# One 512-column matmul for w2's rounded part and its remainder, in a mixture-of-experts kernel

## What is computed

```python
logits = x2d @ wg                     # 2048 tokens, 8 experts
gates = softmax(logits); idx = argmax(logits)
# each expert takes the first C = 256 tokens that chose it
h  = relu(einsum('ecm,emh->ech', di, w1))     # w1: 8 x 256 x 1024
eo = einsum('ech,ehm->ecm', h, w2)            # w2: 8 x 1024 x 256
out = t + combine(gates, eo)
```

## Time and profile before

| | us |
|---|---|
| median of 3 runs | 190.01 (190.01 to 190.08) |
| the profiled execution | 189.76 |
| its span | 187.9 |

### The profile page before, as it was taken

How to read it: one execution, slowest core, us unless ns; L and a number is a source line. 1 busy time by engine, 2 the same in 40 slices (tenths; PEclk the granted TensorE clock), 3 DMA queues, 4 the chain that set the end, 5 groups by cost and what they waited for, 6 DMA issues and landing times.

```text
span 187.9 us, 3937 instructions
## 1 busy us (share of the span) xinstructions
PE 175.9 (94%) x1370; PEld 168.8 (90%) x1370; DVE 147.6 (79%) x400; ACT 112.8 (60%) x273; POOL 119.6 (64%) x159
## 2 busy tenths in 40 slices
PE   7899999799999999989899899999999999999980
PEld 7788898699899999769899899999999999999970
DVE  1397979998987978755867889999699996997820
ACT  0647966578679488523659795791875926845000
POOL 4226778278877967828349688748468494369562
PEclk9999999999999999999999999999999999999996
DMA  5896997611312124769299629139184193601010
GB/s 169 244 368 226 301 258 205 234 61 58 112 36 85 58 86 124 244 179 304 53 330 356 236 79 390 36 127 345 62 284 162 63 348 145 205 22 45 5 68 30
DMA packets 23862, 31.67 MB, mean 169 GB/s; under 512 B 2729, under 2 KB 20650, under 8 KB 23841
## 3 DMA queue, kind: packets, MB, share of 16 engines
q1 hardware_dynamic: 20032, 26.01, 42.5%
q0 software_dynamic: 1616, 4.24, 6.4%
q10 hardware_dynamic: 2192, 1.16, 2.1%
HBM read 23.02 MB, written 8.55 MB: 168 GB/s over the span
## 4 chain that ended last, share of the span: by engine, by line
PE 65%; DVE 12%; DMA 10%; issue 5%; ACT 4%; SPq 2%; POOLq 1%; POOL 0%; DVEq 0%
PE banks_v L603 8%; PE banks_v L604 7%; PE banks_v L610 7%; DMA w_in_sb<-in_L_ffn_w 6%; PE banks_o L675 4%; PE bank_q L610 3%; PE bank_pT L610 3%; PE bank_pT L603 3%; PE bank_pT L604 3%; PE bank_s L610 3%; PE bank_s L603 3%; PE bank_s L604 3%; PE bank_q L603 3%; PE bank_q L604 3%; DMA slots<-row,slot 2%
## 5 line engine op out<-in xcount | busy, mean ns | idle before, releaser
L950 ACT ACTIVATE w_high<-w_in_sb 128x1024 fp32r<-128x1024 f32 x22 | 22.9, 1057 | 4.2 <-DMA w_in_sb<-in_L_ffn_w 4.0
L560 POOL DMA_INDIRECT out<-y,goal x16 | 16.7, 1041 | 11.6 <-issue 5.8
L483 POOL DMA_INDIRECT slots<-row,slot x14 | 14.3, 1023 | 14.7 <-DVE slot L1233 8.8
L542 POOL TENSOR_TENSOR w_low<-vx,w_high 128x1024 fp32r<-128x1024 f32 x8 | 20.1, 2532 | 5.2 <-ACT w_high L950 5.2
L542 POOL TENSOR_TENSOR w_low<-w_in_sb,w_high 128x1024 fp32r<-128x1024 f32 x7 | 16.7, 2409 | 9.7 <-ACT w_high L950 9.6
L1322 DVE TENSOR_TENSOR w_low<-w_in_sb,w_high 128x1024 fp32r<-128x1024 f32 x12 | 15.8, 1317 | 5.1 <-ACT w_high L950 4.7
L603 PE MATMUL banks_v<-w_high,h_high 128*128 128x256 f32 x64 | 16.3, 291 | 0.5 <-issue 0.5
L675 PE MATMUL banks_o<-vx,pT 128*128 128x266 f32 x64 | 16.4, 397 | 0.3 <-issue 0.3
L1048 ACT ACTIVATE h_high<-bank_xT 128x512 fp32r<-128x512 f32 x8 | 4.8, 594 | 18.6 <-PE bank_xT L610 18.6
L604 PE MATMUL banks_v<-w_high,h_low 128*128 128x256 f32 x64 | 15.8, 283 | 0.0
L603 PE MATMUL bank_pT<-w_high,h_high 128*128 128x256 f32 x56 | 14.0, 287 | 0.0
(11 more groups left out here) (239 smaller groups left out, 658.1 us busy)
## 6 DMA issues: line engine op xcount, KB each, us to landing
w_in_sb<-in_L_ffn_w SPq DMA_DIRECT2D x12, 1024.0 KB, 6.6
vx<-in_L_ffn_w SPq DMA_DIRECT2D x4, 1024.0 KB
sl<-slots SPq DMA_DIRECT2D x9, 266.0 KB, 4.2
slots<-empty SPq DMA_DIRECT2D x8, 266.0 KB, 4.1
sl<-in_x SPq DMA_DIRECT2D x8, 256.0 KB, 8.9
out<-row SPq DMA_DIRECT2D x7, 256.0 KB
table_in<-in_tables ACTq DMA_DIRECT2D x1, 292.0 KB, 8.3
w_in_sb<-in_L_conv_Wq ACTq DMA_DIRECT2D x1, 256.0 KB, 4.0
```

What stands on the lines that cost most here:

```text
L483: nc.gpsimd.indirect_dma_start(slot_rows, bass.IndirectOffsetOnAxis(ap=slot_of(i)[:, t:t + 1].bitcast(u32), axis=0), row_of(i)[:, t, :], N ...
L542: step = nc.gpsimd.tensor_tensor(w2_low[e % 2][:, half, :], w2_raw[e % 2][:, half, :], w2_high[e % 2][:, half, :].bitcast(f32), ALU.subtract)
L560: nc.gpsimd.indirect_dma_start(out_rows, bass.IndirectOffsetOnAxis(ap=goal[j][:, c:c + 1].bitcast(u32), axis=0), y[j][:, c, :], None, boun ...
L950: nc.scalar.activation(high[e % 2][:, half, :], raw[:, half, :], ACT.Copy).then_inc(ready, 1)
```

## The change

- w2's high and low parts lie in one buffer, row block by row block side by side (`w2_parts`), so that 512 neighbouring columns hold both.
- `expert_out` no longer uses `three_passes`. For each of the eight blocks it issues one matmul of 512 columns with the high part of h (it gives high x high in the left half of a bank and high x low in the right half), and one of 256 columns with the low part of h into the left half. In the last block the order of the two is turned round. Each tile of 128 tokens has a bank of its own, and the same two banks serve every expert, so the output of e waits for the eviction of e - 1 (`y_ready`).
- The eviction of experts 0 to 6 becomes four operations: for each tile y = right half x gate + own row, then a wait for both, then for each tile y = left half x gate + y.
- The last expert keeps the three passes, in `last_expert_out`; the bank of its second tile is another one.
- `gather_T(1)` stands ahead of the sixth block of expert 0's second tile, and the waits for h's remainders in its first tile stand ahead of the pair of blocks that uses them.

```diff
@@ -195,7 +195,9 @@
         xs = [sb(f"xs{j}", [P, 2, D]) for j in range(2)]
         xg_high, xg_low = ([sb(f"xg_{n}{j}", [P, DC, CAP], f32r) for j in range(2)] for n in ("high", "low"))
         w1_high, w1_low = ([sb(f"w1_{n}{j}", [P, DC, F], f32r) for j in range(2)] for n in ("high", "low"))
-        w2_high, w2_low = ([sb(f"w2_{n}{j}", [P, FC, D], f32r) for j in range(2)] for n in ("high", "low"))
+        w2_parts = [sb(f"w2_parts{j}", [P, FC, 2, D], f32r) for j in range(2)]
+        w2_high, w2_low = ([w[:, :, part, :] for w in w2_parts] for part in range(2))
+        w2_both = [w[:, :, :, :].rearrange("p c a d -> p c (a d)") for w in w2_parts]
         h_high, h_low = ([sb(f"h_{n}{j}", [P, FC, CAP], f32r) for j in range(2)] for n in ("high", "low"))
         y = [sb(f"y{j}", [P, 2, D]) for j in range(2)]
         goal = [sb(f"goal{j}", [P, 2], i32) for j in range(2)]
@@ -226,10 +228,10 @@
         ps_wo_wgc = ps_o[:, 0, 0:DC * EXTRA].rearrange("p (a b) -> p a b", a=DC)
 
         ps_h = [ps_xT, ps_q, ps_s, halves(ps_v[:, 0, :])]
-        ps_y = [halves(ps_v[:, 1, :]), ps_pT]
+        ps_y = [ps_v[:, 1, :], bank_pT[:, :]]
         ps_gT = [halves(ps_o[:, j, :]) for j in range(2)]
 
-        ps_y_last = [ps_gT[0][:, 0, :], ps_y[1][:, 1, :]]
+        ps_y_last = [ps_gT[j][:, 0, :] for j in range(2)]
 
         const_in, eye_in, weights_in, wv_in, small_in, wg_in, token_in = (sem(n) for n in (
             "const_in", "eye_in", "weights_in", "wv_in", "small_in", "wg_in", "token_in"))
@@ -843,21 +845,37 @@
 
             def expert_out(e):
 
-                j, last = e % 2, e == E - 1
+                j = e % 2
                 pe.wait_ge(w2_split, e + 1)
                 if e == 0:
                     pe.wait_ge(first_w2_low, 1)
                 else:
                     pe.wait_ge(h_split, (FC // 2) * (e + 1))
+                    pe.wait_ge(y_ready[1 - j], (e - 1) // 2 + 1)
                 for t in range(2):
                     own = slice(t * P, (t + 1) * P)
-                    step = three_passes(ps_y_last[t] if last else ps_y[j][:, t, :],
-                                        [(h_high[j][:, f, own], h_low[j][:, f, own]) for f in range(FC)],
-                                        [(w2_high[j][:, f, :], w2_low[j][:, f, :]) for f in range(FC)],
-                                        before_last=(lambda: gather_T(1)) if e == 0 and t == 1 else None,
-                                        before_pair=(lambda q: pe.wait_ge(h_split, q + 1)) if e == t == 0 else None)
-                    if last or t == 1:
-                        step.then_inc(y_made, 1)
+                    for f in range(FC):
+                        if e == 0 and t == 0 and f % 2 == 0:
+                            pe.wait_ge(h_split, f // 2 + 1)
+                        if e == 0 and t == 1 and f == FC - 3:
+                            gather_T(1)
+                        high, low, both = h_high[j][:, f, own], h_low[j][:, f, own], w2_both[j][:, f, :]
+                        if f < FC - 1:
+                            nc.tensor.matmul(ps_y[t], high, both, start=f == 0, stop=False)
+                        nc.tensor.matmul(ps_y[t][:, 0:D], low, w2_high[j][:, f, :], start=False, stop=False)
+                        if f == FC - 1:
+                            nc.tensor.matmul(ps_y[t], high, both, start=False, stop=True).then_inc(y_made, 1)
+
+            def last_expert_out():
+
+                e = E - 1
+                j = e % 2
+                pe.wait_ge(w2_split, e + 1)
+                pe.wait_ge(h_split, (FC // 2) * (e + 1))
+                for t in range(2):
+                    own = slice(t * P, (t + 1) * P)
+                    three_passes(ps_y_last[t], [(h_high[j][:, f, own], h_low[j][:, f, own]) for f in range(FC)],
+                                 [(w2_high[j][:, f, :], w2_low[j][:, f, :]) for f in range(FC)]).then_inc(y_made, 1)
 
             hidden(0)
             expert_out(0)
@@ -867,8 +885,7 @@
                 if e + 2 < E:
                     gather_T(e + 2)
                 expert_out(e)
-            pe.wait_ge(y_ready[1], E // 2 - 1)
-            expert_out(E - 1)
+            last_expert_out()
 
 
         @block.scalar
@@ -1337,14 +1354,24 @@
                 gate.done(nc.vector.tensor_tensor(gate_g[:, tiles(e)], ginv[:, tiles(e)], rstd_g[:, tiles(e)], ALU.mult))
                 dve.wait_ge(y_free, e + 1)
                 nc.vector.tensor_copy(goal[j][:, :], sl[:, tiles(e), COL_TOK]).then_inc(goal_ready, 1)
+                if last:
+                    for t in range(2):
+                        dve.wait_ge(y_made, 2 * e + t + 1)
+                        r = 2 * e + t
+                        nc.vector.scalar_tensor_tensor(y[j][:, t, :], ps_y_last[t], gate_g[:, r:r + 1], sl[:, r, 0:D],
+                                                       ALU.mult, ALU.add).then_inc(y_ready[j], 1)
+                    return
                 for t in range(2):
-                    if last or t == 0:
-                        dve.wait_ge(y_made, e + 1 + t)
+                    dve.wait_ge(y_made, 2 * e + t + 1)
                     r = 2 * e + t
-                    step = nc.vector.scalar_tensor_tensor(y[j][:, t, :], ps_y_last[t] if last else ps_y[j][:, t, :], gate_g[:, r:r + 1],
-                                                          sl[:, r, 0:D], ALU.mult, ALU.add)
-                    if last or t == 1:
-                        step.then_inc(y_ready[j], 1)
+                    gate.mark(nc.vector.scalar_tensor_tensor(y[j][:, t, :], ps_y[t][:, D:2 * D], gate_g[:, r:r + 1], sl[:, r, 0:D],
+                                                             ALU.mult, ALU.add))
+                gate.done()
+                for t in range(2):
+                    r = 2 * e + t
+                    step = nc.vector.scalar_tensor_tensor(y[j][:, t, :], ps_y[t][:, 0:D], gate_g[:, r:r + 1], y[j][:, t, :],
+                                                          ALU.mult, ALU.add)
+                step.then_inc(y_ready[j], 1)
 
             first_w2_piece(2)
 
```

## The result

The changed kernel takes 194.1 us (median) where the kernel before took 190.05: the ratio is 1.020, interval 1.015 to 1.025. A second set of runs gave 1.019 (1.011 to 1.027). The median is of four executions, of which one, 196.25 us, ran in a slower state and is left out of the ratio. The profiled execution takes 192.78 us with a span of 191.0, so 3.1 more than the 187.9 of before. It is slower, as forecast; by the ratio the loss is 3.8 us (0.020 x 190.05), where the forecast's sum was 2.6.

A forecast was written before the change was run, and what follows sets the result against it. A ring through DVE, SP, ACT and POOL, slower than PE, was taken as the bound: +0.2 and +2.7 at POOL's last subtraction, +2.6 at PE's start, 192.6 us; 191.5 to 193.7 at 70 in 100, wider range 190.6 to 194.4.

The forecast's parts named there:

- the ring: Loop through DVE's odd evictions, SP's loads, ACT's rounding and POOL's subtraction; a lap took 24.53 and 24.68 us, PE needs 23.90.
- five steps: DVE evicts; POOL's subtraction sets that start; SP's loads wait for the scatter; ACT waits for w1, rounds; POOL subtracts again.
- The eviction: On DVE, experts 0 to 6: two more operations and a wait, 1.76 us instead of 0.86, +0.90 an expert.
- Each odd eviction adds its whole 0.90: Evictions of experts 1, 3 and 5, no slack in the ring: +2.70 us at POOL's last subtraction.
- The start of the ring: First two experts, up to the ring's first step: +0.2 us taken, between ends of -0.6 and +0.9.
- The sum at POOL: End of POOL's last subtraction, for w2 of expert 7: 176.17 + 0.2 + 2.7 = 179.07.
- The wide matmul: PE's expert outputs: 512 columns take 0.2267 us, 0.347 with a narrow one; an expert saves 0.21 us.
- PE waits for POOL at expert 7: Before expert 7's output PE arrives at about 176.8, waits 2.3 us and starts at 179.1 instead of 176.54, +2.6.
- The wait for the banks: PE before expert e's output, for e - 1's eviction: fits for experts 1 to 5, about 0.6 us short for 6.
- PE's wait for the x remainder: At 105.64, behind expert 0's longer eviction on DVE: PE waits until about 106.1, +0.45 us.
- The clock: Rival: PE's idle gap before expert 7 lowers the clock, up to 5.1 us more, 193.7 to 197.7; 10 in 100.
- The even evictions cost nothing: Evictions of even experts stand outside the ring, so their longer time adds nothing at POOL's last subtraction.

The follow-up runs named there:

- second profile: The changed kernel run again without an edit and traced: 194.05 us median, ratio 1.019 (1.011 to 1.027); the profiled execution has a span of 193.0.

## Why the prediction was right, and where not

*The time: inside the range, above the sum.* The median of 194.1 lies between 190.6 and 194.4, but 1.5 above the 192.6 and outside the narrower 191.5 to 193.7. What the profiles show above the sum is the fall of the clock and, in the second, late landings in the ring; both are below. How the executions without a trace share in them is open. The 0.4 us that I gave as what a measurement can tell was too fine: 21 executions of the kernel before lie between 188.81 and 191.65.

*What bounds the kernel: right.* The ring was found in the rows of before, with its five steps. Cutting it at one place returned the kernel to 189.24, and adding only the second pair to the kernel before gave 192.87.

*The eviction: right.* 1.76 was forecast, 1.77 measured.

*Each odd eviction adds its whole 0.90: too much in this execution.* The laps grew by 0.54 and 0.67. Up to the scatter the 0.90 is there: from the eviction's start to the first scatter it took 145.59 - 142.94 = 2.65 us, and 144.44 - 142.70 = 1.74 in the trace of before. But the second scatter ended 1.52 us ahead of SP's loads (148.11 to 149.63), while in the trace of before it was 1.90 (147.03 to 148.93). In the first lap the scatter reported as before (1.53 us for 1.52), but expert 5's w1 came to ACT 7.75 us after its issue (124.96 to 132.71), where it had been 8.00. I had taken every landing time of one execution as a constant, with 0.2 either way. They are what varies: over the eight traces in which SP keeps its wait it is 1.51 to 3.57 us from the end of a scatter to SP, and 7.62 to 8.93 from the load of an odd w1, where it goes right behind that of w2, to ACT. In the second profile the same two laps grew by 0.66 and 1.58. The bounds of the sum should have been taken from that spread.

*The start of the ring: right in its size.* From the start of expert 0's output to the first odd eviction it was 26.67 us before and is 26.89: +0.22, against +0.2. The 0.2 was only the near-middle of -0.6 to +0.9, so that it hit is luck. Expert 0's output itself began 0.52 earlier (90.98 for the 91.50 of the earlier trace rows), in work that the change doesn't touch, so this hid some of the loss. The second profile has 91.78.

*The sum at POOL.* Forecast +2.9. Measured -0.30 for the first odd eviction's place, +0.54, +0.67, and +0.85 for the last eviction and what follows it: +1.76. In the second profile +0.69, +0.66, +1.58 and +0.85: +3.78.

*The wide matmul: the term was mis-sized.* I split a narrow matmul of 0.120 into 0.1067 for columns and 0.0133 fixed, and let a wide one keep one fixed part: 0.2267, 0.347 with a narrow one. It is 0.352, so about 0.232; 8 ns are saved, not 13.3. An expert takes 11.83 instead of 11.95 us: 0.12 saved, not 0.21. The columns' slope from 256 to 274 was no measure for 512. It changed nothing in the forecast, since PE waits. The Trainium skill, "TensorE: Matmul & The Clock Gate", section "Back-to-back issue gap", has 2.5 ns, for an isolated matmul, for what I put at 13.3; the 8 ns of these rows lie between the two.

*PE waits for POOL at expert 7: right.* 1.93 us of idle time for 2.3. The 2.3 does not come out of my own terms: 176.54 + 0.45 - 1.28 + 0.6 is 176.3 for PE, not 176.8, and a wait of 2.8; in the first profile PE was done at 175.66 + 0.39 = 176.05. By the steps of the ring, SP's load went at 149.63 for 151, and ACT's rounding of expert 7's w1 started at 158.05 for 159.2. The wait for the banks was seen as well: none in the first profile's matmuls of experts 1 to 5, and 0.46 us before expert 6 in the second (0.6 was given). PE's wait for the x remainder ended 14.50 us after the start of expert 0's output, 14.14 before: +0.36 for +0.45. The layout cost nothing (POOL's pair 4.75 for 4.77), and the tail is the same: from PE's last matmul to the end of the span 5.5 and 5.4 us.

*The clock: a rival of 10 in 100, and it came in both profiled executions of the kernel after.* The forecast held it improbable since the gap is a little shorter than that of the tail. A last stage under 1.00 was one of its own signs of being wrong. Here the fall followed 1.93 and 1.92 us of idle time, at a cost of 1.6 us (7.51 for 5.92), less than the 5.1 given as its worst, since 1.00 was back at about 181.8. So the profiled execution is near its forecast, 192.78 for 192.4, by luck, as two errors cancel: a ring 1.2 us cheaper, a clock 1.6 us dearer. The chance should have been much higher: the gap was part of my own forecast.

*The even evictions cost nothing: wrong in part.* They cost little as long as the odd ones are the longer; alone with expert 0's they cost 2.2 us, of which 0.9 is expert 0's; for the rest the one trace shows a ring of their own.

## What to carry to other kernels

Before booking a gain on the busiest engine, follow a buffer once around all engines and queues, and compare the lap with that engine's pace: a wait in a queue that issues loads in order can tie an eviction to a weight load two experts later. When a change gives up time on an engine in such a ring, take that wait out first; here the change went from 2% above the kernel before to its time by moving one wait, and to 0.8% below it with two steps exchanged. A forecast that ends in "PE waits about 2 us" must price the clock behind it.

## What was not expected of the hardware

The clock is not settled by the length of the gap. Idle times before expert 7 of 1.92 and 1.93 us were followed by a granted clock of 0.50 for a little over 3 us; 1.45 was not, and neither was 1.91, in the profiled execution with short even evictions (two others of that kernel have a mean of 0.985). Nor does the clock fall inside the gap: PE had begun again at 177.98 and 180.01, and the granted clock was 1.00 until about 178.4 and 180.2.

```profile
178.44 0.39 PE L605 MATMUL banks_o<-w_parts,h_high 128*128 128x256 f32 x1 [1.91 <-POOL w_parts L544]
178.66 0.28 PE L606 MATMUL banks_o<-w_parts,h_low 128*128 128x256 f32 x1
```

```profile
178.00:180.00 2.00, 1.56 (x13) 1.56 (x14) 1.76 (x7) 0.00 (x0) 0.38 (x1) 1.00 0.00 0
```

The Trainium skill, "TensorE: Matmul & The Clock Gate", section "What's actually happening", says that the moment at which the clock rises varies from run to run. It says so of the rise; of the fall these executions show the like, the gap of 1.91 being as long as the two others to 0.02 us.

From the end of a scatter on POOL to the load that SP issues behind it, there are 32 laps in the eight traces in which SP keeps its wait. It took 1.51 to 1.57 us in 25 of them, 1.64 to 2.02 in four, and 2.94, 3.21 and 3.57 in three. Why is open. In a ring such a delay can be kept to the end, as the 2.94 shows.
